# Dealing out anew the preparation of later steps in a three-layer graph network with a closing attention layer

## The chip, the cores and the metric

The kernel runs on one core of a Trainium2 chip. The metric is device time in microseconds of one execution. TensorE is called PE here, VectorE DVE, ScalarE ACT, GpSimd POOL, SyncE SP.

## The reference, cut to what matters

There are 8 graphs of N = 1024 nodes with 256 features and a 0/1 adjacency. Each goes through three layers and one closing attention layer, each step resting on the one before:

```python
h = relu(layernorm(x))                       # raw, at the start
for l in range(3):                           # 24 steps of this kind
    s = leaky_relu(si[:, None] + sj[None, :] + b[l], 0.2)      # si, sj = h @ attn_w[l]
    attn = softmax(where(adj + eye > 0, s, -inf))
    z = layernorm(h + attn @ h) * g1 + beta1
    h = layernorm(z + gelu(z @ W1 + b1) @ W2 + b2) * g2 + beta2
x = x + h
w = relu(layernorm(x)) @ W                   # 8 steps of this kind
out = x + elu(softmax(where(adj == 0, -1e9, leaky_relu(...))) @ w)
```

All is float32 in the inputs; the products of the feed-forward part run as pairs of float16 (a high and a low half).

## The kernel before

`ORDER` lists 32 steps (graph, layer) by hand, so that graphs alternate. A step with layer 3 is a GAT step (6, 10, 14, 18, 22, 29, 30, 31), the others are feed-forward (FFN) steps. Steps 8 to 11, 12 to 15, 16 to 19 and 20 to 23 repeat one pattern. No step waits for an idle machine: while step k runs, the engines prepare step k+1, at times k+2 too. Each engine has its own program in program order, and semaphores tie them together.

One FFN step is, on PE: eight aggregations t = 0 to 7 (`aggregate`: product of the exponentials `pw` with the node values `xx` into the banks OB0 and OB1 by turns, 16 matmuls each), with transposes (`transpose_h` into the bank TH) between them; then sixteen slots n = 0 to 15 with `hidden(n+2)` (6 matmuls into FBB) and `second(n)` (12 matmuls into OB). A GAT step has the eight aggregations alone. On DVE, `residual1(t)` frees OB, `ht_low(j)` makes the low half of a transposed pair and so frees TH, `g_low(n)` makes the low half of the gelu output, which `hidden(n+2)` and `second(n)` wait for, `residual2` takes the result. ACT does `ht_high`, `gelu` (an activation and a copy), the normalisations and exponentials. POOL does the layer norms' scales (`ln_rstd`), `affine` and `final`, the sums into the output.

Preparing a step q takes, in this order: tile scores (`scores(q, t)` on DVE, two operations a tile, lines 1192 and 1197); the score columns, their transpose and copy (`columns`, `transpose_c` into TP, `cT_copy`); `spread_s1` and `spread_sj` on PE, with `r2_copy` on ACT between them; eight row maxima (`row_max` on DVE, line 1250) and after each four the shift columns; eight shifted masks `nms` on ACT (line 919); sixteen units (`unit` on PE: four small products of a mask with the identity into a bank; `score` on DVE, line 1274; `exps` on ACT). Unit u is half u//8 of the nodes, tile u%8. Its bank comes from `score_bank`: R0 and R1 (the halves of RB) by turns, or R0, R1, TH in rotation where `three_banks(q)` holds, as for the GAT steps 10, 14, 18, 22; units 12 to 15 of steps behind a GAT step ("carried", done in the step itself) use TH and TP. A unit in TH waits for the last user of TH to be done (`th_after`).

What stands in which slot is written out in tables: `MAX_*` for row maxima, `SHIFT_*` for masks, `UNITS_*` for units (DVE scores a unit one slot later, `unit_scores`), keyed by slot (t, or 8 + n, or END). `prep_tables` picks them: FE for most steps, FC for steps 9, 13, 17, 21 (in front of a GAT step), FL for late ones, GA for GAT steps in front of an `AHEAD` step (11, 15, 19, 23), TA and TB for the last two. For the AHEAD steps, preparation begins two steps earlier (`MAX_AHEAD`, and the lines with `k + 2 in AHEAD`). `GAT_AT` says in which step the input of an attention layer is prepared: early in 8, 12, 16, 20, 24, 28 (`gat_statistics`, `ln_rstd(LNG)`, `normalise_pair(LNG)`, `gat_transpose`, `gat_low`, `gat_product`, `gat_values`, and `gat_edges`, which puts the diagonal into the mask). In a GAT step, DVE's `elu_a(t)` takes OB, ACT's `elu` makes the exponential and positive part, and POOL's `final` adds both to the output tile; `elu_a(t)` waits for `final(t-2)`.

The lines that the argument touches:

```python
                if t == HT:
                    pe.wait_ge(exp_done, 16 * k + 2 * NT)
...
                    if n in (1, 4) and k not in GAT_FFN_LATE:
                        ht_low(k, 2 + n // 4)
...
                if b == "TH" and th_after:
                    pe.wait_ge(*th_after[-1])
```

## Time and profile before

| | us |
|---|---|
| median of 3 runs | 2446.71 (2444.73 to 2447.41) |
| the profiled execution | 2446.48 |
| its span, first to last instruction | 2444.8 |
| PE busy in it | 2254.4 (92%) |
| DVE busy | 1892.5 (77%) |
| ACT busy | 1572.0 (64%) |
| POOL busy | 1139.1 (47%) |
| mean granted TensorE clock | 0.986 |

The span lies 1.7 us below the execution's own time. The page gives busy times by engine, the span in 40 slices, and the costliest groups of instructions. The view of waits sums for each group how long its engine was idle in front of it and which instruction released it. The order of time lists every instruction, or a merged run of like ones (x16), with its start, its duration and, in brackets, the idle time before it and the releaser. The table of stretches gives each engine's busy time between two times, and the granted TensorE clock (1.00 is 2.4 GHz, half of it 1.2 GHz). Step 12 runs from 1007.9, step 13 from 1096.7, step 14 from 1181.1, step 15 from 1216.3 to 1297.9 us of the span; step 29 begins at 2313.1, step 30 at 2364.6, step 31 at 2409.9.

### The profile page before, as it was taken

How to read it: one execution, taken by the hardware profiler on the slowest of the kernel's cores; microseconds unless marked ns; L12 is line 12 of the kernel's file. 1: busy time of each engine (PE TensorE's matmuls, PEld its weight loads, DVE VectorE, ACT ScalarE, POOL GpSimd, SP SyncE). 2: the span in 40 equal slices, each digit the busy share in tenths (PEclk: the TensorE clock that was granted, in tenths of full speed). 3: DMA queues.
4: the chain of work that ended last, by engine and by line, in shares of the span. 5: the costliest groups of instructions: out<-in, count | busy, mean ns of one | idle time of the engine just before them, and what ended most of it. 6: DMA issues, size and time to landing. Idle time of an engine off the chain costs nothing.

```text
span 2444.8 us, 41401 instructions
## 1 busy us (share of the span) xinstructions
PE 2254.4 (92%) x14623; PEld 1711.6 (70%) x14623; DVE 1892.5 (77%) x5043; ACT 1572.0 (64%) x2450; POOL 1139.1 (47%) x2128
## 2 busy tenths in 40 slices
PE   5889999998899999999899999999998999999988
PEld 4666766776667767767777767777675777677667
DVE  7777778758788887888887788978878677767875
ACT  5467566666666676676766666766656557666754
POOL 3344346354264543644546444554544445335643
PEclk9899999999999999999999999999999999999989
DMA  6312012011130112200121102111131010010000
GB/s 217 120 44 90 6 61 78 11 51 48 48 113 1 44 48 83 78 19 26 64 84 61 44 5 91 60 53 44 40 108 56 6 44 10 5 40 23 23 25 29
DMA packets 66221, 128.55 MB, mean 53 GB/s; under 512 B 12985, under 2 KB 53213, under 8 KB 62942
## 3 DMA queue, kind: packets, MB, share of 16 engines
q1 hardware_dynamic: 66014, 125.90, 15.4%
q8 instruction: 116, 1.90, 0.3%
q14 instruction: 91, 0.75, 0.1%
HBM read 111.20 MB, written 14.68 MB: 51 GB/s over the span
## 4 chain that ended last, share of the span: by engine, by line
PE 61%; DVE 26%; issue 5%; POOL 4%; ACT 3%; DMA 1%; SPq 0%; DVEq 0%; POOLq 0%; ACTq 0%
PE OB L1639 40%; PE FBB L1639 13%; DVE mj L1250 5%; DVE pw L1274 4%; PE RB L1639 4%; DVE gT L1288 3%; DVE st L1141 2%; DVE junk L1192 2%; PE TH L1639 2%; DVE xc L1168 1%; DVE junk L1197 1%; PE TH L1680 1%; POOL xc L676 1%; DVE xc L1155 1%; DMA adjst<-in_adj 1%
## 5 line engine op out<-in xcount | busy, mean ns | idle before, releaser
L1639 PE MATMUL OB<-xx,pw 128*128 128x257 f32 x4096 | 947.2, 386 | 22.7 <-DVE xc L1168 10.9
L1639 PEld LDWEIGHTS OB<-xx,pw 128*128 128x128 f32 x4096 | 770.3, 192 | 149.9 <-DVE xc L1168 16.8
L1639 PE MATMUL FBB<-hT,wb 128*128 128x512 f16 x2304 | 563.1, 383 | 55.1 <-DVE gT L1288 54.3
L1639 PE MATMUL OB<-wb,gT 128*128 128x256 f16 x4608 | 572.4, 275 | 10.1 <-DVE gT L1288 10.1
L1639 PEld LDWEIGHTS OB<-wb,gT 128*128 128x128 f16 x4608 | 453.4, 99 | 141.3 <-DVE gT L1288 12.6
L649 POOL TENSOR_SCALAR ve<-mv 128x2 f32<-128x2 f32 x256 | 59.5, 233 | 1026.5 <-DVE mv L1144 1018.1
L891 ACT ACTIVATE FBB<-FBB,wc 128x512 f32<-128x512 f32 x384 | 252.2, 657 | 292.3 <-PE FBB L1639 291.7
L1639 PEld LDWEIGHTS FBB<-hT,wb 128*128 128x128 f16 x2304 | 214.0, 98 | 265.7 <-DVE gT L1288 66.6
L1288 DVE TENSOR_TENSOR gT<-FBB,gT 128x512 f16<-128x512 f32 x384 | 262.0, 683 | 171.9 <-ACT gT L896 171.7
L902 ACT ACTIVATE pw<-pw,sj 128x512 f32<-128x512 f32 x512 | 334.1, 710 | 59.7 <-DVE pw L1274 58.9
L676 POOL TENSOR_TENSOR xc<-xc,gb 128x256 f32<-128x256 f32 x384 | 292.0, 760 | 33.5 <-ACT xc L866 32.4
L919 ACT ACTIVATE nms<-nm,cc 128x1024 bf16<-128x1024 bf16 x256 | 282.3, 1137 | 19.0 <-DVE cc L1265 19.0
L866 ACT ACTIVATE xc<-xc,nb,rs 128x256 f32<-128x256 f32 x384 | 212.4, 590 | 104.8 <-POOL nb L657 104.5
L1274 DVE SCALAR_TENSOR_TENSOR pw<-r2s,sj,RB 128x512 f32<-128x512 f32 x377 | 268.4, 738 | 3.5 <-PE RB L1639 3.3
L1250 DVE CUSTOM_DVE_ANT_0 mj<-RB,nm 128x1024 bf16<-128x1024 f32 x224 | 267.2, 1215 | 0.0
L896 ACT ACTIVATE gT<-FBB 128x512 f16<-128x512 f32 x384 | 229.3, 597 | 12.1
L654 POOL TENSOR_TENSOR rs<-ve,mhalf 128x2 f32<-128x2 f32 x256 | 183.6, 717 | 21.3
L1151 DVE RECIPROCAL rden<-OB 128x1 f32<-128x1 f32 x192 | 32.0, 166 | 204.7 <-PE OB L1639 203.7
L1639 PE MATMUL RB<-identb,nms 128*128 128x128 bf16 x1508 | 134.9, 224 | 34.8 <-DVE pw L1274 29.3
L1141 DVE BATCH_NORM_STATS2 st<-xc 128x6 f32<-128x256 f32 x392 | 156.7, 421 | 6.8
L678 POOL TENSOR_TENSOR xx<-xc,gb 128x256 f32<-128x256 f32 x192 | 147.8, 770 | 15.1
L1197 DVE CUSTOM_DVE_ANT_0 junk<-xx,aw 128x256 bf16<-128x256 f32 x256 | 154.6, 604 | 0.0
(141 smaller groups left out, 2334.0 us busy)
## 6 DMA issues: line engine op xcount, KB each, us to landing
wb<-w_scratch SPq DMA_DIRECT2D x19, 2048.0 KB, 7.9
adjst<-in_adj SPq DMA_DIRECT2D x56, 512.0 KB, 4.1
xx<-in_x SPq DMA_DIRECT2D x16, 512.0 KB, 5.7
nm<-in_L_gnn_W SPq DMA_DIRECT2D x6, 1024.0 KB, 8.5
gb<-in_L_gnn_g SPq DMA_DIRECT2D x48, 128.0 KB, 2.8
adjst<-in_x SPq DMA_DIRECT2D x6, 1024.0 KB, 10.9
out_x<-adjst SPq DMA_DIRECT2D x48, 128.0 KB, 1.7
pw<-in_adj SPq DMA_DIRECT2D x4, 1024.0 KB, 9.6
```

Source lines behind the costliest of these rows:

```text
L654: pool.tensor_tensor(out=rs[:, kind, c], in0=ve[:, kind, c], in1=mhalf[:, :], op=ALU.pow)\
L676: pool.tensor_tensor(out=v, in0=v, in1=gb[:, 0, :], op=ALU.mult).then_inc(mul_done[kind], 1)
L866: act.activation(dst, src, ACT.Relu if kind in (LNR, LNG) else ACT.Identity, bias=nb[:, kind, t:t + 1], scale=rs[:, kind, t:t + 1])\
L891: act.activation(src, src, ACT.Gelu, bias=b1c[:, layer(k), f:f + 1], scale=1.0 / W_SCALE)\
L896: act.activation(gT[:, i % GRING, 0, :], src, ACT.Copy).then_inc(ghi_done, 1)
L902: act.activation(v, v, ACT.Exp, bias=sj2[:, q % 2, jt:jt + 1]).then_inc(exp_done, 1)
L919: act.activation(nms[:, it, :], nm[:, slot(q), it, :], ACT.Identity, bias=cc[:, it:it + 1])\
L1141: dve.bn_stats(st[:, kind, t % 2, :], src[:, t, 0:D]).then_inc(bs_done[kind], 1)
L1250: dve.tensor_tensor_reduce(out=mj[:, n % 2, :], in0=row_bank(q)[:, :], in1=nm[:, g % 3, t, :], scale=1.0, scalar=-3e38, op0=ALU.add, op1=A ...
L1274: dve.scalar_tensor_tensor(out=pw[:, jt, half], in0=r2s[:, half], scalar=sj8[:, q % 2, jt:jt + 1], in1=b, op0=ALU.max, op1=ALU.add).then_i ...
L1288: dve.tensor_tensor(out=gT[:, i % GRING, 1, :], in0=FB[i % 2][:, :], in1=gT[:, i % GRING, 0, :], op=ALU.subtract).then_inc(glo_odd if n % ...
L1639: return pe.matmul(o, lhsT, rhs, start=first, stop=last)
```

## The change

It is a new dealing of the same work over slots and engines, in these parts.

1. Steps in front of a GAT step (FC): row maximum 5 a slot earlier, masks from the fourth on and all units a slot earlier.
2. AHEAD steps: all eight tile scores in t = 0 to 5 two steps before (four of them were in n = 1, 3, 5, 7), columns, copies, spreads and row maxima a slot earlier, maxima 6 and 7 at the end of that step and no longer in the GAT step; in the GAT step the other tile scores one a tile at first, and the units from t = 3.
3. Unit 13 of an AHEAD step goes to the bank R0; the next step's spread waits for its score.
4. The diagonal masks (`gat_edges`) go from n = 3 into the aggregation, t = 4. POOL's LNG scale comes ahead of the affine operations, ACT's first LNG pair from n = 2 to n = 3.
5. `g_low(2)` directly behind `ht_low(2)` at n = 1; at n = 8 the scores before the residuals.
6. The aggregation waits for each exponential of the second half alone.
7. Step 29: DVE makes the sum of the ELU's two parts (`elu_b`), the last GAT product and its low half come behind the units and their scores, the last exponentials ahead of the last values. Step 30: unit 15 a tile later.

```diff
--- before.py
+++ after.py
@@ -57,6 +57,7 @@
 GAT_AT = {5: 0, 8: 1, 12: 2, 16: 3, 20: 4, 24: 5, 28: 6, 29: 7}
+ELU_DVE = {29}
 LATE = {2, 3, 4, 26, 27, 28}
@@ -88,15 +89,14 @@
 MAX_FE = {2: (0,), 3: (1,), 4: (2,), 5: (3,), 6: (4,), 7: (5,), 8: (6,), 9: (7,)}
-MAX_FC = {2: (0,), 3: (1,), 4: (2,), 5: (3,), 6: (4,), 7: (5, 6), 8: (7,)}
+MAX_FC = {2: (0,), 3: (1,), 4: (2,), 5: (3,), 6: (4, 5), 7: (6,), 8: (7,)}
 MAX_GX = {2: (0, 1), 3: (2, 3), 4: (4, 5), 5: (6, 7)}
...
 MAX_GE = {3: (0,), 4: (1, 2), 5: (3, 4), 6: (5, 6), 7: (7,)}
-MAX_AHEAD = {21: (0,), 22: (1, 2), 23: (3,), END: (4, 5)}
-MAX_GA = {0: (6,), 1: (7,)}
+MAX_AHEAD = {20: (0,), 21: (1, 2), 22: (3,), 23: (4, 5), END: (6, 7)}
 ALL8 = tuple(range(NT))
@@ -107,7 +107,7 @@
 UNITS_FG = {23: (0, 1), END: (2, 3, 4, 5, 6, 7)}
-UNITS_FC = {11: (0, 1), 12: (2, 3), 13: (4, 5), 14: (6, 7), 15: (8, 9), 16: (10, 11), 17: (12, 13, 14, 15)}
+UNITS_FC = {10: (0, 1), 11: (2, 3), 12: (4, 5), 13: (6, 7), 14: (8, 9), 15: (10, 11, 12), 16: (13, 14, 15)}
 MAX_TA = {1: (0,), 2: (1, 2), 3: (3, 4), 4: (5,), 5: (6,), 6: (7,)}
@@ -122,14 +122,14 @@
 UNITS_GE = {END: TO12}
-UNITS_GA = {4: (0, 1), 5: (2, 3), 6: (4, 5), 7: (6, 7), END: (8, 9, 10, 11)}
+UNITS_GA = {3: (0, 1), 4: (2, 3), 5: (4, 5), 6: (6, 7), END: (8, 9, 10, 11)}
...
 SHIFT_FG = {21: (0, 1), 22: (2, 3), END: (4, 5, 6, 7)}
-SHIFT_FC = {6: (0, 1), 7: (2,), 10: (3,), 11: (4,), 12: (5,), 13: (6,), 14: (7,)}
+SHIFT_FC = {6: (0, 1), 7: (2,), 9: (3,), 10: (4,), 11: (5,), 12: (6,), 13: (7,)}
 SHIFT_GE = {6: (0, 1), 7: (2, 3), END: (4, 5, 6, 7)}
@@ -149,7 +149,7 @@
     if v == "ahead":
-        return dict(col=None, ct=None, s1=None, sj=None, row=MAX_GA, units=UNITS_GA, shift=SHIFT_GA)
+        return dict(col=None, ct=None, s1=None, sj=None, row={}, units=UNITS_GA, shift=SHIFT_GA)
     if v == "early":
@@ -176,7 +176,7 @@
     if k == 30:
-        return {1: (8, 9, 10, 11), 2: (12, 13, 14, 15)}
+        return {1: (8, 9, 10, 11), 2: (12, 13, 14), 3: (15,)}
     if k == 31:
@@ -197,6 +197,8 @@
         return ("TH", "TP")[u % 2] if u in (8, 9, 12, 13) else ("R0", "R1")[u % 2]
+    if q in AHEAD and u == 13:
+        return "R0"
     if q in CARRY and u in (8, 9, 12, 13, 14, 15):
@@ -695,9 +697,10 @@
                 v = x1_of(g)[:, t, :]
-                pool.wait_ge(elu_exp, n)
-                pool.tensor_tensor(out=v, in0=v, in1=vn[:, t % 2, :], op=ALU.add).then_inc(elu_sum, 1)
-                pool.wait_ge(elu_max, n)
+                if k not in ELU_DVE:
+                    pool.wait_ge(elu_exp, n)
+                    pool.tensor_tensor(out=v, in0=v, in1=vn[:, t % 2, :], op=ALU.add).then_inc(elu_sum, 1)
+                    pool.wait_ge(elu_max, n)
                 pool.wait_ge(elu_sum, n)
@@ -742,6 +745,8 @@
                         ln_rstd(LNR, raw, n // 2)
+                    if gat is not None and early and n in (1, 3, 5, 7):
+                        ln_rstd(LNG, gat, n // 2)
                     if n in (1, 3, 9, 11):
@@ -758,8 +763,6 @@
                             self_edges(raw, n - 2)
-                    if gat is not None and early and n in (1, 3, 5, 7):
-                        ln_rstd(LNG, gat, n // 2)
                     if n == 12:
@@ -1035,11 +1038,11 @@
                         normalise_pair(LNR, raw, (5, 7, 8, 9).index(n))
-                    if k + 2 in AHEAD and n == 12:
+                    if k + 2 in AHEAD and n == 11:
                         r2_copy(k + 2)
                     if gat is not None and early:
-                        if n in (2, 4, 6, 8):
-                            if n == 2:
+                        if n in (3, 4, 6, 8):
+                            if n == 3:
                                 act.wait_ge(max_done, 8 * (k + 1) + 8)
@@ -1082,11 +1085,9 @@
                     gat_pair(gat, 3)
-                    exps(k + 1, 2)
-                    exps(k + 1, 3)
+                    for u in range(2, NT):
+                        exps(k + 1, u)
                     gat_values(gat, 3)
-                    for u in range(4, NT):
-                        exps(k + 1, u)
                     shifts(k, END)
@@ -1352,6 +1353,14 @@
+            def elu_b(k, t):
+
+                n = 8 * ORDER[k][0] + t + 1
+                dve.wait_ge(elu_exp, n)
+                dve.wait_ge(elu_max, n)
+                dve.tensor_tensor(out=va[:, t % 2, :], in0=vn[:, t % 2, :], in1=va[:, t % 2, :], op=ALU.add)\
+                   .then_inc(elu_sum, 1)
+
             def piece_low(i):
@@ -1379,9 +1388,11 @@
                 elif is_gat(k) and k + 1 in AHEAD:
-                    tiles = {0: (0, 1), 1: (2, 3), 2: (4, 5), 3: (6, 7)}.get(at, ())
+                    tiles = {0: (0,), 1: (1,), 2: (2, 3), 3: (4,), 4: (5,), 5: (6,), 6: (7,)}.get(at, ())
                 elif k + 1 in LATE:
                     tiles = {2: (4, 5), 3: (6, 7)}.get(at, ())
+                elif k + 2 in AHEAD:
+                    tiles = {0: (0, 1), 1: (2, 3), 2: (4,), 3: (5,), 4: (6,), 5: (7,)}.get(at, ())
                 else:
@@ -1445,9 +1456,11 @@
                         gat_statistics(gat, t - 5)
+                    if gat is not None and early and t == 4:
+                        gat_edges(gat)
                 g_low(k, 1)
                 for n in range(NF):
-                    if n > 1:
+                    if n > 1 and (n > 2 or k in GAT_FFN_LATE):
                         g_low(k, n)
@@ -1467,19 +1480,21 @@
                         ht_low(k, 2 + n // 4)
+                    if n == 1 and k not in GAT_FFN_LATE:
+                        g_low(k, 2)
                     if k < 2 and n == 7:
...
                         piece_low(2 * k + n // 14)
+                    unit_scores(k, 8 + n)
                     if n == 8:
...
                             residual2(k, t)
-                    unit_scores(k, 8 + n)
                     prepare(k, 8 + n)
                     if k + 2 in AHEAD:
-                        if n == 8:
+                        if n == 7:
                             columns(k + 2)
-                        if n == 10:
+                        if n == 9:
                             cT_copy(k + 2)
@@ -1509,14 +1524,10 @@
                             gat_low(gat, (n - 5) // 2)
-                        if n == 3:
-                            gat_edges(gat)
                         if n == 13 and gat == 6:
...
                             scores(GAT_STEP[gat], n - 8)
-                    if k + 2 in AHEAD and n in (1, 3, 5, 7):
-                        scores(k + 2, n // 2)
                     if nxt is not None and n >= 14 and k + 2 not in AHEAD and k + 3 not in AHEAD \
@@ -1547,6 +1558,8 @@
                     elu_a(k, t)
+                    if k in ELU_DVE and t >= 1:
+                        elu_b(k, t - 1)
                     if gat is not None and t in (1, 2, 4, 5):
@@ -1566,9 +1579,11 @@
                         gat_sum(7)
+                if k in ELU_DVE:
+                    elu_b(k, NT - 1)
                 if gat is not None:
+                    finish(k)
                     gat_low(gat, 3)
-                    finish(k)
                     for t in range(HT):
@@ -1662,11 +1677,9 @@
                 rows = slice(t * P, (t + 1) * P)
-                if t == HT:
-                    pe.wait_ge(exp_done, 16 * k + 2 * NT)
                 for jt in nodes:
-                    if t == 0:
-                        pe.wait_ge(exp_done, 16 * k + jt + 1)
+                    if t % HT == 0:
+                        pe.wait_ge(exp_done, 16 * k + NT * (t // HT) + jt + 1)
                     ins = mm(o[:, 0:D + 1], pw[:, jt, rows], xx[:, s, jt, 0:D + 1], jt == 0, jt == NT - 1)
@@ -1751,7 +1764,7 @@
                 if q > 0:
-                    pe.wait_ge(x_done, 16 * q - (4 if q - 1 in CARRY and q - 1 not in RB_CARRY else 0))
+                    pe.wait_ge(x_done, 16 * q - (2 if q - 1 in AHEAD else 4 if q - 1 in CARRY and q - 1 not in RB_CARRY else 0))
                 spread(1, row1_done, RB)
@@ -1866,11 +1879,11 @@
                     if k + 2 in AHEAD:
-                        if n == 9:
+                        if n == 8:
                             transpose_c(k + 2)
+                        if n == 10:
+                            spread_s1(k + 2)
                         if n == 11:
-                            spread_s1(k + 2)
-                        if n == 12:
                             spread_sj(k + 2)
@@ -1911,9 +1924,9 @@
                         gat_colsum(7)
+                prepare(k, END)
                 if gat is not None:
                     gat_product(gat, 3)
-                prepare(k, END)
...
             pe.wait_ge(zero_done, 2)
```

## Rows read from the trace of the kernel before

**Rows 1.** The page, engines: busy us (share of the span) x instructions

```profile
PE 2254.4 (92%) x14623; PEld 1711.6 (70%) x14623; DVE 1892.5 (77%) x5043; ACT 1572.0 (64%) x2450; POOL 1139.1 (47%) x2128
```

**Rows 2.** PE waits, whole span: us in total, times, longest

```profile
PE FBB L1639 <- DVE gT L1288: 54.3, 48, 3.9
...
PE OB L1639 <- ACT pw L902: 3.3, 2, 2.5
```

**Rows 3.** Steps 13 and 14: length; busy PE, PEld, DVE, ACT, POOL; clock, DMA, GB/s

```profile
1096.70:1181.10 84.40, 79.99 (x532) 59.17 (x532) 66.74 (x177) 53.66 (x83) 38.64 (x71) 1.00 0.10 32
1181.10:1216.30 35.20, 31.70 (x177) 26.62 (x177) 31.38 (x95) 28.90 (x49) 20.65 (x32) 1.00 0.24 86
```

**Rows 4.** PE waits in step 12 (1007.9 to 1096.7), columns as above

```profile
PE FBB L1639 <- DVE gT L1288: 2.3, 2, 1.9
PE RB L1639 <- DVE pw L1274: 1.4, 1, 1.4
...
PE TP L1798 <- DVE mj L1325: 0.3, 1, 0.3
```

**Rows 5.** Order of time, step 12: start, us, engine, what [idle before <-releaser]

```profile
1048.50 0.68 DVE L1288 TENSOR_TENSOR gT<-FBB,gT 128x512 f16<-128x512 f32 x1
...
1050.25 1.09 ACT L866 ACTIVATE mj<-adjst,nb,rs 128x256 f32<-128x256 f32 x2 [3.79 <-POOL nb L657]
...
1053.35 2.19 DVE L1319 SCALAR_TENSOR_TENSOR nm<-ident,dgm,nm 128x128 bf16<-128x128 f32 x8
```

**Rows 6.** Order of time, PE in step 13

```profile
1104.55 0.61 PE L1639 MATMUL RB<-cT,sel 32*128 32x128 bf16 x8
...
1138.21 1.47 PE L1639 MATMUL FBB<-hT,wb 128*128 128x512 f16 x6 [1.22 <-DVE gT L1288]
...
1143.88 0.39 PE L1639 MATMUL TH<-identb,nms 128*128 128x128 bf16 x4
...
1157.76 0.40 PE L1639 MATMUL TH<-identb,nms 128*128 128x128 bf16 x4 [1.29 <-DVE pw L1274]
...
1162.30 0.40 PE L1639 MATMUL RB<-identb,nms 128*128 128x128 bf16 x4 [0.86 <-DVE pw L1274]
```

**Rows 7.** All of line 1192 (min/median/max ns), then order of time, DVE and ACT

```profile
L1192 DVE CUSTOM_DVE_ANT_0 junk<-xx,aw x256: 407/422/985, 10.2 to 2376.0; 128x256 bf16<-128x256 f32 x128
...
1102.09 0.18 DVE L1225 COPY cT<-TP 64x128 bf16<-64x128 bf16 x1
...
1135.49 0.63 ACT L891 ACTIVATE FBB<-FBB,wc 128x512 f32<-128x512 f32 x1
...
1141.65 0.68 DVE L1282 TENSOR_TENSOR hT<-TH,hT 128x512 f16<-128x512 f32 x1
```

**Rows 8.** Order of time, PE and ACT in step 14

```profile
1181.13 14.16 PE L1639 MATMUL OB<-xx,pw 128*128 128x257 f32 x64 [0.77 <-DVE xc L1168]
...
1194.35 2.17 ACT L919 ACTIVATE nms<-nm,cc 128x1024 bf16<-128x1024 bf16 x2
...
1197.27 3.74 PE L1639 MATMUL OB<-xx,pw 128*128 128x257 f32 x16 [1.98 <-DVE hT L1345]
...
1215.41 0.40 PE L1639 MATMUL RB<-identb,nms 128*128 128x128 bf16 x4 [0.87 <-DVE pw L1274]
```

**Rows 9.** Order of time, PE in step 15

```profile
1221.55 0.40 PE L1639 MATMUL TP<-identb,nms 128*128 128x128 bf16 x4 [1.06 <-DVE cT L1225]
```

**Rows 10.** Order of time, PE in step 26

```profile
2102.78 1.47 PE L1639 MATMUL FBB<-hT,wb 128*128 128x512 f16 x6 [1.03 <-DVE gT L1288]
...
2105.67 1.47 PE L1639 MATMUL FBB<-hT,wb 128*128 128x512 f16 x6
```

**Rows 11.** Order of time, PE in steps 29 and 30

```profile
2359.66 2.74 PE L1639 MATMUL TH<-gw,wb 128*128 128x256 f16 x12 [2.67 <-DVE wb L1325]
...
2379.33 0.40 PE L1639 MATMUL TH<-identb,nms 128*128 128x128 bf16 x4 [2.51 <-DVE pw L1274]
...
2379.83 5.42 PE L1639 MATMUL OB<-xx,pw 128*128 128x257 f32 x16
```

## Prediction

> **What bounds the kernel now.** I read the page first. PE is busy 92% of the span, 190 us short of it [rows 1], so the kernel is a PE stream with holes and a change can gain only what it takes out of the holes. The total of PE's waits then says whose they are: most are waits for DVE (the low half of the gelu output, gT, 54.3 us in 48 waits), 3.3 us in two waits are for ACT's exponentials [rows 2]. The steps repeat: 8 to 11, 12 to 15, 16 to 19 and 20 to 23 are one cycle, which I read at 12 to 15; the table of stretches gives steps 13 and 14 as 84.40 and 35.20 us with PE busy 79.99 and 31.70 [rows 3], so 4.4 and 3.5 us are idle. Then I went through the order of time at each hole. Below, t is an aggregation tile, n one of the 16 slots of the feed-forward part, and a gain is a hole that goes less the hole that comes next. PE, DVE, ACT and POOL each run in program order, so a moved line moves all that stands behind it.
>
> **Steps with an early attention layer in preparation (8, 12, 16, 20, 28; 24 alike).** Before, DVE does the row maximum and the shift columns in front of gT for n=2, at 1048.50, and PE waits 1.9 us for it [rows 4, 5]. ACT stands 3.79 us for POOL's LNG scale in front of gelu 3, then DVE spends 2.19 us on the diagonal masks (eight operations) in front of gT 4 and the first scores, and PE waits 0.4 and 1.4 us more [rows 4, 5]. After: gT 2 comes straight behind hT's low half, at 1046.7, so PE goes on at 1047.2 (1.9 gone). POOL makes the LNG scale ahead of the four affine operations, ACT's pair moves behind gelu 3. But that pair now ends near 1051.2, since gelu 3, one hT copy and a shifted mask (waiting for the shift columns, near 1049.0) stand ahead of it, and PE, at the transposes by 1050.3, waits 0.9. The first scores are ready at 54.4, PE wants a bank at 54.2: 0.25. DVE then reaches the low half of the transposed x late, as before (0.3 of wait [rows 4]), and I put 0.95. Old 1.9+0.4+1.4+0.3 = 4.0, new 2.1: 1.9 each. The masks now lie at t=4, where DVE waited for PE about 1 us a tile: 2.4 us more make the low half for n=0 end at about 36.9 where PE wants it at 36.8, so 0.1 at most; without that cover it would be 2.4. Six steps give 11.4 us. Bounds: 0.5 (the wait only moves, see the rivals) to 2.8 each.
>
> **Steps 9, 13, 17, 21.** Removed: 1.22 (gT 2 stood behind tile scores), 1.29 (the scores of n=8 stood behind the residuals, which wait for PE) and 0.86 (the next bank behind those) [rows 6], 3.37 us. Added, two things. (a) Four tile scores come into t=0 and 1 of DVE, in front of the cT copy, which ends at 1102.3 [rows 7] and which the next spread, at 1104.55 [rows 6], needs. POOL runs its affine operations just then; one such operation takes 0.42 us in the median and up to 0.985 [rows 7], and the long ones lie beside POOL's additions. Two tiles, four operations: about 1.4 us if none is long (they overlap a little), about 2.9 if three are, as in step 14's like stretch. The copy then ends near 1105.2: a wait of 0.65. Behind it on DVE are three constants and the residual of t=1, not wanted soon.
> (b) The units of step 14 are dealt one slot earlier, so unit 2 stands at n=3 in PE. It uses the bank TH, and TH holds the fourth transpose pair until DVE's ht_low(3), which stays at n=4, behind g_low(4). In the trace before, that copy runs at 1141.65 [rows 7] and unit 2 comes at 1143.88 without a wait [rows 6]. After, counting from 1133.3: PE ends second(2) at about 1139.4 and meets unit 2. ACT makes a shifted mask (1.1) at n=2, then gelu 3 (two operations, 1.3), the hT copy (0.6), a mask (1.1), gelu 4 (1.3), from 1135.6 (gelu 3 starts at 1135.49 today, and two masks take 2.17 [rows 7, 8]): 1140.9. Then DVE g_low(4) and ht_low(3), 0.6 each: 1142.1. PE waits **2.7 us** with hidden(5), second(3) and all the rest queued behind it. Bounds: 1.5 (ACT does a mask less in front) and 3.9 (the longest gT wait of the whole trace [rows 2]). Nothing in the diff moves ht_low(3).
> Gone 3.37, come 3.35: zero. But the two waits of this length in the last steps, 2.67 and 2.51 us, are each followed by matmuls at 1.2 GHz, sixteen in 5.42 us [rows 11] instead of the 3.74 of a tile at 2.4 GHz [rows 8]: 1.7 us. Waits of 1.98 and less in this cycle have a full granted clock behind them [rows 3, 8] (step 14's stretch has 1.00). I take 1.7 for all four: **6.8 us lost**; ends 0 and 4 x 3.4.
>
> The Trainium skill's GPSIMD Engine Reference (section Specifications) says that POOL shares its SBUF interfaces with DVE and contends with DVE instructions that have two SBUF inputs, as the tile scores have; it speaks against moving them under the affine operations. The 0.985 beside 0.42 agrees [rows 7]. Without contention (a) is nothing and the sum is 2.6 us lower.
>
> **Steps 10, 14, 18, 22.** Removed: 1.98 us at tile 4, where OB waits for the third elu_a behind two row maxima and four tile scores of DVE [rows 8], and 0.87 at the end, with two of 0.26 beside it (R0 and R1 wait for scores), 3.37 together. Row maxima 6 and 7 go in front of elu_a(0), which no longer delays PE before t=2. Added: PE meets units 0 and 1 after tile 3, at about 1195.5, while ACT ends the shifted mask for rows 2 and 3 at 1196.5 [rows 8]: 0.85. Tile 4 then ends at 1200.5, and units 2 and 3 find their banks free at about 1201.5 and 1202.1, as elu_a(2) waits for POOL's first final until 1194.6 and pushes the scores back: near 0.9 beyond PE's own time. At the start DVE has two row maxima (2.3) in n=15 instead of one and the shift columns (1.8), so the 0.77 in front of tile 0 [rows 8] grows by 0.35. 3.37 - 0.85 - 0.9 - 0.35 = 1.3; by a chain that counts DVE's uncontended times it is 2.1; I take 1.6: 6.4 us. Bounds 0 and 2.2.
>
> **Steps 11, 15, 19.** Unit 13 goes to R0 and no longer waits 1.06 us for cT [rows 9]: 3.2 us. The spread of t=1 now waits for score 13, about 1 us early. Step 23 has no such transpose.
>
> **Step 0 and step 7.** The aggregation waits for each exponential alone. The two waits were 3.3 us [rows 2]; the last two tiles are wanted 2.6 us later than the first, so both go: 3.3. Step 7 also had the longest gT wait, 3.9, in front of n=2; gT 3 stays where it is on DVE, so of it about 1.5 remain gained. 4.8 together; ends 2 and 7.
>
> **Other late steps.** In 2, 3, 4, 25, 26, 27 the wait (1.03 in step 26 [rows 10]) in front of hidden(4) goes as well, but hidden(5) there starts at 2105.67, right behind gT 3 [rows 10], which DVE does no sooner: zero.
>
> **Steps 29 and 30.** In 29 the product waits 2.67 us and runs at half clock [rows 11]; the four units and their scores go in front of it, and what is left is about 1.7 of wait: 2.2 us. ELU sums on DVE (eight at about 0.4) take as many of 0.73 off POOL, whose final holds elu_a back: 0.2. In 30 unit 15 waited 2.51 us in TH for unit 12's score; a tile later it finds the bank free and its exponential is ready 1 us before tile 4 wants it. With the half clock behind it: 2.5+1.7, less 0.3: 3.9. Together 6.3; ends 2 and 8.
>
> **The sum.** 11.4 - 6.8 + 6.4 + 3.2 + 4.8 + 0 + 6.3 = 25.3 us off the profiled execution of 2446.48, whose span of 2444.8 is 1.7 shorter. It is 0.2 below the median of 2446.71, which changes nothing. **2421 us**, 1.0% less.
>
> **Rivals.**
> (1) The wait at unit 2 comes but the clock stays up, as behind the 1.98: +6.8 gained, 2414. For it: 2.7 is close to the limit between the kinds. Against: both waits over 2.5 near the end have the slow stretch.
> (2) The holes only move, as in step 26 [rows 10]: gT 2 is early and PE stands again one slot later, since ACT's gelu 3 and the chain of the transposes set the pace. Six steps give 0.5 instead of 1.9 and step 7 nothing: 2431.
> (3) As (2), and the GAT steps give nothing since ACT, which is busy through tiles 0 to 3, is the bound there: 2437 to 2441, hardly to be told from no change.
> (4) Slower. TH is the bound of steps 9, 13, 17, 21: unit 2 and, one slot on, unit 5 both meet it late, each as long as the longest wait (3.9 [rows 2]) and each with 3.4 us lost to a slow clock twice as long. 2 x 7.3 + 0.65 - 3.37 = 11.9 a step, 47.5 in all against 32.1 of the other terms: 2462. It decides from 8 us a step. Against it: unit 5 only needs score 2, one slot earlier on DVE, which has nothing else there.
>
> **Chances.** The forecast 0.45, (1) 0.2, (2) 0.2, (3) 0.08, (4) 0.07. The range reaches from (1) with the better ends of the GAT steps and of step 30 to (3): 2405 to 2440. What a measurement of this kernel can tell from no change is about 0.2%, 4.9 us: under 2441.8 is faster. Faster 0.87, within 0.07, slower 0.06.
>
> **What would show it.** Right: a PE wait of 2 to 3 us in front of four matmuls TH<-identb,nms at about n=3 of steps 9, 13, 17, 21, with the granted clock of the stretch below 1.00; step 14 near 33.6 us with no wait at tile 4; step 12 near 87; step 15 near 80.5; no wait of PE on TP in it; step 30 four us shorter. Wrong: no wait at TH (then step 13 is 3 us shorter), or a wait before hidden(5) in step 12 as long as the one that went.

## The result and the profile after

The changed kernel takes 2409.22 us (median of 4, 2407.82 to 2414.69) against 2445.72 for the kernel before (4 runs, 2441.23 to 2447.41): a ratio of 0.9865, interval 0.985 to 0.988, 1.35% faster. The profiled execution took 2410.06, so 36.4 us went, where I had 25.3. The page's engine line, to be held against [rows 1]:

```profile
PE 2246.6 (93%) x14623; PEld 1707.8 (71%) x14623; DVE 1896.2 (79%) x5051; ACT 1572.4 (65%) x2450; POOL 1130.3 (47%) x2120
```

PE is still the stream that counts; of the span's 36.5 us 28.7 are idle time gone and 7.8 busy time. Of the busy time 4.6 are half-clock stretches (8.8 us less busy time in steps 5, 7, 24, 29 and 30, 4.2 more in 9, 13 and 17); the rest are 0.1 to 0.4 us in many steps. PE's waits over the whole span (in all, times, longest) say whose idle time it was:

```profile
PE FBB L1654 <- DVE gT L1289: 35.6, 27, 4.0
PE RB L1654 <- DVE pw L1275: 17.9, 30, 4.2
PE OB L1654 <- DVE xc L1169: 13.7, 21, 1.5
...
PE TH L1654 <- DVE hT L1283: 12.1, 5, 2.5
```

The waits for gT fell from 54.3 us in 48 to 35.6 in 27 [rows 2]. New is the last line, of which the kernel before had one wait of 0.4 us: five waits of units for `ht_low`, four of them my wait at unit 2, the fifth in step 7. In the stretches of steps 12, 13, 14, 21 and 23 (length; busy PE, PEld, DVE, ACT, POOL; clock, DMA share, GB/s) the two in the middle answer to [rows 3]:

```profile
993.90:1080.20 86.30, 84.55 (x577) 64.59 (x577) 67.86 (x184) 58.91 (x95) 44.07 (x88) 1.00 0.14 44
1080.20:1166.80 86.60, 81.45 (x532) 59.64 (x532) 70.46 (x181) 54.95 (x85) 38.91 (x71) 0.98 0.11 34
1166.80:1199.50 32.70, 31.32 (x177) 26.65 (x177) 27.76 (x89) 27.61 (x45) 19.22 (x30) 1.00 0.22 87
...
1651.80:1736.80 85.00, 79.83 (x533) 59.14 (x533) 70.45 (x181) 55.01 (x85) 38.93 (x71) 1.00 0.10 35
1769.40:1860.00 90.60, 79.62 (x518) 58.62 (x515) 67.67 (x170) 52.59 (x83) 39.45 (x75) 0.98 0.21 66
```

Step 13 is 2.2 us longer than before and its clock below 1.00; step 14 is 2.5 shorter. Read so from the first aggregation of each step to that of the next, the 36.4 us lie here:

| steps | forecast | measured |
|---|---|---|
| 8, 12, 16, 20 (-2.4 each), 24 (-2.7), 28 (-3.9) | -11.4 | -16.3 |
| 9, 13, 17 (+2.0, +2.2, +2.2), 21 (+0.5) | +6.8 | +6.9 |
| 10, 14, 18, 22 | -6.4 | -10.1 |
| 11, 15, 19 | -3.2 | -3.8 |
| 23 | 0 | +2.4 |
| 0 and 7 | -4.8 | -4.9 |
| 29 and 30 | -6.3 | -5.5 |
| in front of step 0 (-1.7), 3 (-1.8), 4 (-0.8), 5 (-0.9) | 0 | -5.2 |

PE's holes in steps 13 and 14, with what ended them:

```profile
1089.13 0.61 PE L1654 MATMUL RB<-cT,sel 32*128 32x128 bf16 x8 [1.00 <-DVE cT L1226]
...
1126.64 0.40 PE L1654 MATMUL TH<-identb,nms 128*128 128x128 bf16 x4 [2.41 <-DVE hT L1283]
...
1127.17 2.76 PE L1654 MATMUL FBB<-hT,wb 128*128 128x512 f16 x6
...
1166.83 14.16 PE L1654 MATMUL OB<-xx,pw 128*128 128x257 f32 x64 [1.47 <-DVE xc L1169]
1181.42 0.61 PE L1654 MATMUL RB<-identb,nms 128*128 128x128 bf16 x8 [0.43 <-ACT nms L922]
1186.22 0.40 PE L1654 MATMUL RB<-identb,nms 128*128 128x128 bf16 x4 [0.67 <-DVE pw L1275]
```

The three waits of [rows 6] are gone; unit 2 waits 2.41 us in TH, and the six matmuls behind it take 2.76 us instead of 1.47. In step 21 the same wait has the full clock behind it, hence 85.0 instead of 86.6: the stretch costs 1.67 us. At tile 4 of step 14 nothing is left of the 1.98 [rows 8].

In step 7, which the change touches too, the wait of 3.85 us for gT in the kernel before has become two:

```profile
667.57 1.47 PE L1654 MATMUL FBB<-hT,wb 128*128 128x512 f16 x6 [2.36 <-DVE gT L1289]
...
672.85 0.47 PE L1654 MATMUL TH<-identb,nms 128*128 128x128 bf16 x4 [2.50 <-DVE hT L1283]
```

### The profile page after: what moved, and what is told of

Same layout as the page of the kernel before. It is cut to its first block, busy times and chain, and to the rows that moved or that the text cites. A ratio compares the mean times of both kernels' runs of the same rounds, so it can differ in the third digit from the quotient of the medians.

```text
span 2408.3 us, 41405 instructions
## 1 busy us (share of the span) xinstructions
PE 2246.6 (93%) x14623; PEld 1707.8 (71%) x14623; DVE 1896.2 (79%) x5051; ACT 1572.4 (65%) x2450; POOL 1130.3 (47%) x2120
## 4 chain that ended last, share of the span: by engine, by line
PE 55%; DVE 27%; issue 6%; ACT 5%; POOL 5%; DMA 2%; SPq 0%; DVEq 0%; POOLq 0%; ACTq 0%
PE OB L1654 36%; PE FBB L1654 11%; DVE mj L1251 5%; DVE pw L1275 4%; PE RB L1654 4%; DVE gT L1289 3%; DVE st L1142 3%; PE TH L1654 2%; DVE junk L1193 2%; DMA adjst<-in_adj 1%; ACT nms L922 1%; DVE xc L1169 1%; DVE nm L1300 1%; DVE xc L1156 1%; POOL xc L678 1%
## 5 line engine op out<-in xcount | busy, mean ns | idle before, releaser
L1654 PE MATMUL OB<-xx,pw 128*128 128x257 f32 x4096 | 942.5, 385 | 16.0 <-DVE xc L1169 13.7
L1654 PE MATMUL FBB<-hT,wb 128*128 128x512 f16 x2304 | 566.8, 384 | 36.8 <-DVE gT L1289 35.6
L1654 PE MATMUL OB<-wb,gT 128*128 128x256 f16 x4608 | 572.7, 275 | 10.2 <-DVE gT L1289 10.1
L678 POOL TENSOR_TENSOR xc<-xc,gb 128x256 f32<-128x256 f32 x384 | 290.8, 757 | 42.7 <-ACT xc L869 41.9
L680 POOL TENSOR_TENSOR xc<-xc,gb 128x256 f32<-128x256 f32 x192 | 144.3, 751 | 15.1
## 6 DMA issues: line engine op xcount, KB each, us to landing
pw<-in_adj SPq DMA_DIRECT2D x4, 1024.0 KB, 10.4
```

The source lines that it names most:

```text
L678: pool.tensor_tensor(out=v, in0=v, in1=gb[:, 0, :], op=ALU.mult).then_inc(mul_done[kind], 1)
L680: pool.tensor_tensor(out=o, in0=v, in1=gb[:, 1, :], op=ALU.add).then_inc(aff_done[kind], 1)
L1654: return pe.matmul(o, lhsT, rhs, start=first, stop=last)
```

## The experiments

A whole kernel's time moves by 1 to 3 us with the half-clock stretches that it happens to catch, most in steps 0, 3, 5 and 23, and by 1.7 us with the time in front of step 0 (explained in the last section). So I read steps, and beside their length PE's idle time in them. In most steps that a kernel leaves alone, the idle time repeats within 0.2 us. It doesn't in step 0 (12.3 to 13.7), step 3 (8.4 to 9.8), step 5 (10.9 to 11.6), step 6 (3.0 to 3.5), step 11 (2.0 to 2.3) and step 23 (10.4 to 11.6). The four kernels with mixed parts (two sections of undone parts, one of done parts, one last mix) ran once each, at 2424.67, 2416.15, 2434.07 and 2411.97 us in the order of this text, and their steps are read from that one execution.

**Unit 2's bank.** The first theory to test: the wait is for TH, and the slow clock is its consequence.

```diff
-                    if n in (1, 4) and k not in GAT_FFN_LATE:
-                        ht_low(k, 2 + n // 4)
+                    if n in (1, 3 if k + 2 in AHEAD else 4) and k not in GAT_FFN_LATE:
+                        ht_low(k, 2 + (n > 1))
```

> The changed kernel, with DVE's last low half of the transpose pair (the copy that frees bank TH) made one slot earlier (n=3 instead of n=4) in steps 9, 13, 17 and 21 alone. Theory (the wait of 2.41 us in front of unit 2 is for that copy, and the half-clock stretch behind it belongs to that wait): the wait at unit 2 goes to under 0.3 us, the slow stretches of steps 9, 13, 17 go with it, steps 9, 13, 17 are 3.8 to 4.2 us shorter (from 86.4-86.6 to about 82.4), step 21 is 2.2 to 2.5 us shorter (from 84.9 to 82.6), the whole about 14 us shorter: near 2395. Rival A (the copy is a bystander; the hole only moves to the next gT, in front of the hidden product of n=5): the wait at unit 2 goes, another of 1.5 us or more appears within two slots, the steps are at most 1 us shorter, the clock may or may not stay up. Rival B (the slow stretch is not tied to that wait): the steps are 2.4 us shorter, yet a half-clock stretch of the same length still stands in steps 9, 13, 17: near 2400.

2397.92 us, ratio to before 0.9809 (0.979 to 0.983). Steps 9, 13, 17 and 21 take 82.6 us, 3.8, 4.0, 4.0 and 2.3 less: 14.0 in all. The medians differ by 11.3 only; in the profiled executions the time in front of step 0 took 1.7 back. In order of time step 13 has only these two holes and the one of 0.26 before `second`:

```profile
1086.62 0.61 PE L1654 MATMUL RB<-cT,sel 32*128 32x128 bf16 x8 [1.01 <-DVE cT L1226]
...
1160.35 0.92 PE L1654 MATMUL OB<-xx,pw 128*128 128x257 f32 x3 [1.47 <-DVE xc L1169]
```

The theory holds, both rivals fall. With that one line moved the four steps are 7.1 us shorter than in the kernel before; with it left where it was they were 6.9 longer.

**The column copy behind the tile scores.** At slot t=1 of the same steps, with `first = k + 2 in AHEAD and tabs["ct"] == at`:

```diff
+                if first:
+                    cT_copy(k + 1)
+                    constants(k + 1)
                 tile_scores(k, at)
-                if tabs["ct"] == at:
+                if tabs["ct"] == at and not first:
```

> The changed kernel, with DVE's copy of the transposed column sums and the three constants made in front of the two tile scores at t=1 of steps 9, 13, 17, 21. Theory (the wait of 1.00 us in front of the spread of row 1 is for that copy, which stands behind four tile-score operations slowed to 0.9 us beside POOL's affine operations): the wait at the spread falls from 1.00 to under 0.2 us and each of the four steps is 0.8 to 1.0 us shorter, 3.5 to 4 us in all: near 2405.5. Rival (the delay comes back): the tile scores end one or two us later, the score transposes for the next units or the low half of the gelu output are late by the same time, and the steps keep their length within 0.3 us: near 2409.

2407.35 us, 0.9845 (0.983 to 0.986). The wait at the spread is gone and PE's idle time falls from 5.15 to 4.13 us in all four steps; lengths 85.5, then 83.8 three times. So 1.0 a step, as expected; that is read from the idle time, since the medians differ by 1.9 only. That steps 13 and 17 show 2.8 is the slow clock, which did not come this time behind the same 2.41 us. DVE's operations in the changed kernel show why the copy was late:

```profile
1085.62 0.70 DVE L1193 CUSTOM_DVE_ANT_0 junk<-xx,aw 128x256 bf16<-128x256 f32 x1
...
1086.26 0.94 DVE L1198 CUSTOM_DVE_ANT_0 junk<-xx,aw 128x256 bf16<-128x256 f32 x1
...
1087.13 0.94 DVE L1193 CUSTOM_DVE_ANT_0 junk<-xx,aw 128x256 bf16<-128x256 f32 x1
...
1088.87 0.21 DVE L1226 COPY cT<-TP 64x128 bf16<-64x128 bf16 x1
```

POOL runs its affine operations from 1085.32 to 1092.0, and beside them a tile score takes 0.94 us, against the median of 0.42 [rows 7]. Over the whole changed kernel 117 of 512 such operations take more than 0.7 us, and all 117 run beside a POOL operation on two tensors of 256 columns; the 173 that run while POOL is idle take 0.41 to 0.43.

**Step 23, first try.** Statistics and edges of the raw graph's tiles 0 and 1 together at t=1:

```diff
-                        if t % 2 == 0:
-                            raw_statistics(raw, t // 2)
-                        edges(raw, t)
+                        if k == 23 and t < 2:
+                            if t == 1:
+                                raw_statistics(raw, 0)
+                                edges(raw, 0)
+                                edges(raw, 1)
```

> The changed kernel, with DVE's statistics and edge terms of the first raw layer input in step 23 taken at t=1 together, behind the maxima and scores of t=0, instead of at t=0 and t=1. Theory (step 23 grew by 2.4 us because DVE, which runs ahead after the change, meets the raw input before its load has landed, idles 5 us there, and hands the hole on: PE waits 2.33 us at tile 3 and 3.97 in front of a hidden product): DVE's idle time of 5 us goes, PE's wait at tile 3 goes to under 0.5, and step 23 is 2 to 2.5 us shorter (from 90.6 to about 88.3): near 2407. Rival A (the load lands late in any order): DVE idles the same time one tile later, step 23 stays within 0.5 us of 90.6. Rival B (step 23 grew because its other half-clock stretch is longer): the tile-3 wait goes, the step stays at 89.5 or more.

2413.39 us, 0.9873 (0.986 to 0.989). A miss. The wait of 2.33 at tile 3 goes, and DVE waits 1.41 us for the load instead of 4.98, but PE meets another directly behind that tile, and step 23 is 90.2 us (idle 11.03 instead of 10.98):

```profile
1790.72 0.66 PE L1699 MATMUL TH<-ident,xc 128*128 128x128 f32 x4 [3.34 <-ACT xc L869]
```

Rival A holds: the load lands late in any order, and most of the wait only stands elsewhere, on ACT and PE. In the next kernel this edit goes along with the two before and with row maximum 5 at the end of the step:

```diff
-MAX_AHEAD = {20: (0,), 21: (1, 2), 22: (3,), 23: (4, 5), END: (6, 7)}
+MAX_AHEAD = {20: (0,), 21: (1, 2), 22: (3,), 23: (4,), END: (5, 6, 7)}
```

> The changed kernel with the three edits of the runs before it (low half of the pair at n=3, column copy in front of tile scores, raw statistics of step 23 at t=1) and, in steps 9, 13, 17, 21, row maximum 5 of the attention layer moved from slot n=15 to the end of the step, behind what tile 0 of the next step waits for. Theory: the three edits hit different holes, so their gains add: 14 + 3.7 + 2.3 us; the moved maximum takes the wait of 1.47 us in front of tile 0 of steps 10, 14, 18, 22 down to about 0.8, 2.5 us in all: 2409 - 22.5 = near 2387. Rival (the holes are one chain through DVE, and what is taken out of one comes back at the next): less than 14 us in all, near 2396, with a wait at tile 4 of the attention steps of over 1 us that the changed kernel does not have.

2386.99 us, 0.9766 (0.975 to 0.978). Steps 9, 13, 17 and 21 take 80.4 us with 0.7 idle, steps 10, 14, 18 and 22 take 32.35 (32.66 in the changed kernel). The gains add; that step 23 gives nothing is made up for by the tile-0 wait, which falls to 0.32 instead of 0.8.

**One part undone per step.** Since the steps repeat, each can carry its own undone part, and one run gives many differences. In this kernel, among others (ten steps are changed in all):

```diff
-                    if n > 1 and (n > 2 or k in GAT_FFN_LATE):
+                    if n > 1 and (n > 2 or k in GAT_FFN_LATE or k in (8, 12)):
...
-                    if gat is not None and early and t == 4:
+                    if gat is not None and early and t == 4 and k not in (8, 16):
...
-                        if n in (3, 4, 6, 8):
+                        if n in (2 if k in (8, 20) else 3, 4, 6, 8):
...
+                elif k == 22:
+                    tiles = {0: (0, 1), 1: (2, 3), 2: (4, 5), 3: (6, 7)}.get(at, ())
```

> The changed kernel with one part put back in each of ten separate steps, read by the length of each step against the changed kernel's. Theory (each part hits its own hole): step 12 (gT 2 back at n=2) +1.9 us; step 16 (diagonal masks back at n=3) +1.0; step 20 (LNG scale of POOL and first ACT pair back where they were) +0.5; step 8 (all three back) +2.4; step 14 (row maxima 6 and 7 back in front of the first two elu_a) +1.0, made of a shorter wait at tile 0 and a new one at tile 4; step 18 (units one tile later) +0.9 at its end; step 22 (tile scores two a tile) +0.3; step 11 (unit 13 back in TP) +1.0; step 0 (exponentials awaited all at once at tile 4) +1.8; step 29 (elu sums on POOL) +0.2; step 30 (unit 15 back with unit 14) +3.5, with a half-clock stretch. Rival (one chain: the three edits of step 12 work only together): each of steps 12, 16 and 20 alone loses nearly the whole 2.4 us, or each loses under 0.3 and only step 8 the 2.4.

Step lengths against the changed kernel, idle time of PE in brackets:

| step, part undone | expected | measured |
|---|---|---|
| 12, gT 2 | +1.9 | 0.0 (1.77 to 2.02) |
| 16, masks | +1.0 | +0.45 |
| 20, LNG order | +0.5 | +2.8 (1.77 to 4.26) |
| 8, all three | +2.4 | +2.4 |
| 22, tile scores | +0.3 | +3.0 (1.36 to 4.08) |
| 14, row maxima | +1.0 | -0.3; step 13 idle 5.15 to 4.18 |
| 18, units a tile later | +0.9 | +0.1 |
| 11, unit 13 in TP | +1.0 | +1.8 (2.25 to 3.74) |
| 0, exponentials | +1.8 | +0.9 (12.3 to 15.7, untouched up to 13.7) |
| 29, elu sums | +0.2 | -0.7 (7.19 to 6.99) |
| 30, unit 15 | +3.5 | +2.3 (3.21 to 4.40) |

Neither theory nor rival holds: the three edits of step 12 don't share its gain, one has most of it. In step 20, with POOL's LNG scale behind the affine operations again, ACT and PE stand as in the kernel before [rows 4, 5], although gT 2 is early there:

```profile
1615.36 1.09 ACT L874 ACTIVATE mj<-adjst,nb,rs 128x256 f32<-128x256 f32 x2 [3.79 <-POOL nb L662]
```

```profile
1616.50 0.66 PE L1822 MATMUL TP<-ident,mj 128*128 128x128 f32 x4 [1.05 <-ACT mj L874]
1618.40 1.47 PE L1663 MATMUL FBB<-hT,wb 128*128 128x512 f16 x6 [1.24 <-DVE gT L1294]
1622.35 0.40 PE L1663 MATMUL RB<-identb,nms 128*128 128x128 bf16 x4 [1.18 <-DVE pw L1280]
```

In step 12, with gT 2 late, one wait takes the place of the two at TP (0.97 and 0.54) and the step is as long:

```profile
1045.68 1.47 PE L1663 MATMUL FBB<-hT,wb 128*128 128x512 f16 x6 [1.76 <-DVE gT L1294]
```

**A second mix**, with for instance

```diff
+                    if k != 17:
+                        unit_scores(k, 8 + n)
                     if n == 8:
                         for t in range(HT):
                             residual2(k, t)
-                    unit_scores(k, 8 + n)
+                    if k == 17:
+                        unit_scores(k, 8 + n)
```

> The changed kernel with one part put back in each of eight steps, read by step length. Theory: step 13 (units and shifted masks of the next step one slot later) loses the wait of 2.41 us in front of unit 2 and with it any half-clock stretch, and stays under 83.5 us; step 17 (residuals back in front of the unit scores of n=8) +1.3 us; step 9 (row maxima 4 and 5 apart) within 0.2; step 21 (tile scores back at n=1, 3, 5, 7 instead of t=0, 1) loses the 1.00 at the spread and gets 0.5 to 1.2 in front of the hidden products; step 3 (gT 2 back at n=2) +1.8, step 7 +1.9, step 26 within 0.2, since there gT 3 sets the start of the next hidden product in any order; step 29 (PE's product before the units again) +2.0. Rival for step 13: the wait is not for bank TH but for PE's place in a longer chain; then it stands one slot later and the step stays above 85. Rival for step 3: its gain of 1.8 came from elsewhere and it stays at 88.8.

Step 13, units and masks a slot later: the 2.41 goes and no half-clock stretch is left, idle 5.15 to 3.89. The step takes 83.8 us, 0.3 more than I had, for a wait of 0.85 comes at a bank RB. Step 17, residuals in front: +2.6, with a wait of 1.51 and two of 0.26, twice what I had. Step 9: +0.1. Step 21, tile scores back in the slots n: the wait at the spread goes, that at unit 2 grows from 2.41 to 2.99, idle 5.15 to 4.72; with a half-clock stretch behind it the step is 1.0 longer. Step 3, gT 2: length +0.2, which says little there, as its idle time moves by more from kernel to kernel. Steps 7 and 26, gT 2: nothing (-0.05 and 0.0); 26 as forecast, 7 not. In step 7 the wait for gT is 3.86 again and that in TH falls to 0.25. Step 29, the product first again: +1.6 (idle +0.8).

**The raw load, second try.** SP issues it ahead of the attention step's last store; the stores are counted in halves (`out_lo`, `out_done`):

```diff
                     for t in range(NT):
+                        if t == NT - 1 and RAW_AT.get(k + 1, 0) >= 3:
+                            sp.wait_ge(agg_done, 8 * k + 8)
+                            load_x(RAW_AT[k + 1])
+                            sp.wait_ge(out_lo, 64 * (g + 1))
+                            load_adj(RAW_AT[k + 1], 0)
                         sp.wait_ge(o_ready, 8 * g + t + 1)
```

> The changed kernel, with SyncE issuing the load of the next raw graph (and its first adjacency tile) in front of the last store of the attention step's output instead of behind it, after the aggregation of that step; stores counted in two halves so that the first adjacency tile waits only for the first four. Theory (step 23 is 2.4 us longer than before because the changed attention step ends sooner for TensorE while its last output, POOL's, does not, so the load behind that store starts 5.7 us into step 23 instead of 2.3): the load lands 4 to 6 us earlier in step 23, VectorE's idle of 4.98 us is under 1, the wait of 2.33 at tile 3 goes, and step 23 is 2.4 to 3.5 us shorter, under 88.2; steps 7, 11, 15, 19, where the raw input is wanted later, do not change: near 2406.5. Rival (what bounds step 23 is the 3.97 us wait in front of a hidden product, which does not come from the load): VectorE's idle time goes but the step stays above 89.5.

2408.49 us, 0.9854 (0.984 to 0.987). Step 23 takes 86.7 us instead of 90.6, idle 7.71 instead of 10.98; from step 4 on no other step's idle time moves by more than 0.3. The whole kernel shows little of it (0.7 us by the medians). POOL's last output and SP's queue in the changed kernel (step 23 starts at 1769.4), then SP's of this one (at 1772.1):

```profile
1771.13 0.73 POOL L705 TENSOR_TENSOR adjst<-adjst,hT 128x256 f32<-128x256 f32 x1
```

```profile
1771.89 0.33 SPq L599 DMA_DIRECT2D out_x<-adjst  x1
...
1775.08 0.93 SPq L475 DMA_DIRECT2D xx<-in_x  x2
```

```profile
1771.39 0.94 SPq L476 DMA_DIRECT2D xx<-in_x  x2
...
1774.57 0.36 SPq L606 DMA_DIRECT2D out_x<-adjst  x1
```

The load stood 5.7 us into the step and stands 0.7 ahead of it now. DVE, which waited for it in the changed kernel

```profile
1780.78 0.75 DVE L1142 BATCH_NORM_STATS2 st<-xx 128x6 f32<-128x256 f32 x2 [4.98 <-DMA xx<-in_x]
```

has no wait for it left, and PE none at tile 3. The wait in front of `hidden(5)`, 3.98 us, is untouched. So 3.9 us is more than the 2.4 that the change had cost. With the edits at TH, at the copy and at the row maximum, but not the moved statistics:

> The best kernel so far (transpose pair's low half at n=3, column copy first, row maximum 5 at the end of the step), with the earlier raw load in place of the moved raw statistics. Theory: as the kernel with all parts, 2387, less what step 23 gets back, 2.5 to 4 us: near 2383.5. Rival: step 23 keeps its length, 2387.

**2382.54 us** (5 runs, 2380.26 to 2383.22), 0.9744 (0.973 to 0.976) of before, 26.7 us less than the changed kernel: the best version of this study. Its steps 13, 14 and 23:

```profile
1074.00:1154.40 80.40, 79.69 (x532) 59.16 (x532) 68.95 (x179) 53.70 (x83) 38.88 (x71) 1.00 0.10 34
1154.40:1186.80 32.40, 31.26 (x177) 26.61 (x177) 28.31 (x91) 28.56 (x47) 19.55 (x30) 1.00 0.26 94
...
1745.50:1832.20 86.70, 79.00 (x517) 58.68 (x514) 67.50 (x170) 52.64 (x83) 38.79 (x75) 0.98 0.22 69
```

**One part done per step,** on top of the kernel before, so that a part's worth alone and its worth within the change can be told apart. In step 12 POOL's LNG scale ahead of the affine operations, the rest alike:

```diff
+                    if gat is not None and early and n in (1, 3, 5, 7) and k in (8, 12, 28):
+                        ln_rstd(LNG, gat, n // 2)
                     if n in (1, 3, 9, 11):
...
-                        if n in (2, 4, 6, 8):
+                        if n in (3 if k in (8, 12, 28) else 2, 4, 6, 8):
```

> The kernel before, with one part of the change made in each of several separate steps, read by step length against the kernel before (the counterpart of the first mixed kernel, which undid them). Theory A (what undoing showed: the order of the LNG scale carries the gain of the steps with an early attention layer, gT 2 and the masks little): step 12 (LNG order alone) -2.0 to -2.4 us, step 28 (LNG order alone) -2 to -3.9, step 16 (gT 2 alone) within 0.3, step 20 (masks at t=4 alone) within 0.5, step 8 (LNG order and gT 2) as step 12, step 24 and step 3 (gT 2 alone) within 0.5 and about -0.7. Theory B (my prediction's attribution): step 16 -1.9, step 12 -0.5, step 20 -1.0. Further, by undoing: step 22 (tile scores dealt over seven tiles) -2 to -3 with the 1.98 us wait at tile 4 gone, step 14 (units of the next step one tile sooner) within 0.3, steps 17 and 18 (columns and row maxima of the attention layer sooner, 6 and 7 out of the first two elu_a) between -0.5 and +1 together, step 11 (unit 13 in bank R0) -1.0 or more, step 9 (unit scores in front of the residuals) -1.3 to -2.5, step 13 (units and shifted masks sooner, nothing else) +1 to +3 with the wait of 2.4 us in front of unit 2, step 7 (exponentials one by one) -0.8.

| step, the one part | length before | now |
|---|---|---|
| 12, LNG order | 88.81 | 86.78 |
| 16, gT 2 | 88.80 | 88.81 |
| 20, masks | 88.80 | 89.15 |
| 8, LNG order and gT 2 | 88.80 | 86.80 |
| 22, tile scores over seven tiles | 35.16 | 32.58 |
| 14, units a tile sooner | 35.17 | 36.30 |
| 17 and 18, columns and row maxima | 119.57 | 120.03 |
| 11, unit 13 in R0 | 81.51 | 80.43 |
| 9, scores ahead of residuals | 84.41 | 83.09 |
| 13, units and masks a slot sooner | 84.41 | 85.83 |
| 7, exponentials one by one | 94.40 | 91.28 |
| 3, gT 2 | 90.56 | 88.74 |
| 24, gT 2 | 96.68 | 96.67 |
| 28, LNG order | 92.14 | 90.96 |

Theory A holds in steps 8, 12, 16, 20, 22 and 24; B falls. Steps 9, 11, 13 and 17 with 18 lie in their forecasts too, but in step 13 the wait at unit 2 is 1.64, not 2.4, since the 1.22 for gT still stands in front of it, and the clock stays up. Three are misses: step 14 is 1.1 longer, with waits of 1.38 for a mask and 3.15 at a bank RB; step 7 is 3.1 shorter, of which 1.2 are idle time and most of the rest a half-clock stretch that stood behind waits of 1.08 and 0.79 us; step 28 is only 1.2 shorter. Step 3 is 1.8 shorter with gT 2 alone (idle 10.50 to 8.80), more than A had, but undone it had cost only 0.2. In step 28 2.2 us of idle time go and a half-clock stretch comes.

**A last mix of undone parts**: the units of step 22 a tile later, row maxima of 17/18 back, LNG order back in 28 and, with gT 2, in 12, masks back in 24:

```diff
-        return dict(col=None, ct=None, s1=None, sj=None, row={}, units=UNITS_GA, shift=SHIFT_GA)
+        return dict(col=None, ct=None, s1=None, sj=None, row=MAX_GA if q == 19 else {},
+                    units=UNITS_GA0 if q == 23 else UNITS_GA, shift=SHIFT_GA)
```

> The changed kernel with one part put back in each of five places. Theory: step 22 with the next step's first units one tile later again: step 22 within 0.2 us, but step 23 2.0 to 2.5 us shorter, because taking two units out of the end of the step had brought step 23's start 2 us nearer to POOL's last output, behind which the raw load stands (the load is issued 5.7 us into step 23 now, then near 3.5). Rival: the load's lateness comes from the tile scores and stays; step 23 within 0.5 of 90.6. Steps 17 and 18 with the row maxima as before: together 1.0 to 1.3 us shorter (without counting a half-clock stretch, 1.7, that may stand in step 17 or not). Step 28 with the LNG scale's order alone put back: +2.5 to +3.9, the two row maxima of this step included; step 12 with LNG order and gT 2 both put back, masks new: +2.4 to +2.8, all of what step 20 with the LNG order alone showed; step 24 with the masks back: +0.4 if they are what they are in step 16, +2 or more if they carry what the order of LNG, not used in step 24, cannot have brought.

Step 22 +0.1; in step 23 the load is issued 2.3 us in (5.7), and PE's idle time falls from 10.98 to 9.47. The length falls by only 0.6, since a second half-clock stretch stands in the step. So the cause is told apart from the tile scores. Its size, 1.5, shows only in the idle time, which in this step moves by up to 0.6 in kernels that leave it alone. Steps 17 and 18: idle 5.15 to 4.18 and 1.35 to 1.38, so the new row maxima cost 1.0 us a cycle. Step 12 +2.8. Step 28 +3.4, of it 1.6 idle. Step 24 is 1.0 us **shorter** with the masks at n=3 (idle 6.61 to 5.66), outside both cases that I had named.

## Why the prediction was right or wrong

**Step 12 and its like**, 16.3 where I had 11.4 (2.4 each, 3.9 in step 28). The list of waits was right and their owner wrong. I gave 1.9 to gT 2; moved alone it brings 0.0, undone it costs 0.0. The row that I had and priced too low was ACT's 3.79 us for POOL's LNG scale [rows 5]. With that wait, gelu 3 and all behind it are 2 to 3 us late whatever DVE does, and the time that PE gains at gT 2 it gives back at TP and at `hidden(5)`; I had seen just that in step 26 and not carried it over. The LNG order alone brings 2.0, and 2.8 in a kernel with the other two parts in it. The masks bring 0.45 behind that order and cost 0.35 alone. At t=4 of step 24, which I had called alike, they cost 1.0: DVE has row maxima in those tiles, has no idle time from the masks at 1888 until 1905, and PE gets waits of 0.54 and 0.91 us that go when the masks are back at n=3. In the last mix I took the LNG order to have no part in step 24. That was wrong: ACT stood 3.80 us for POOL there before the change and doesn't behind it, and gT 2 alone is worth 0.0 and the masks are a loss, so that order is the likely source of the 2.7. No run moved it alone in this step.

**Steps 9, 13, 17, 21**, +6.9 where I had +6.8: the wait at unit 2, its cause (the bank TH, `ht_low(3)` a slot too late) and the clock behind it came as worked out, 2.41 for 2.7. The copy's wait was 1.00 for 0.65, since all operations behind the first ran slowed. Four at the uncontended 0.42 would have let the copy go near 1087.1 (an estimate), ahead of 1088.1, where PE wanted it. The Trainium skill's GPSIMD Engine Reference (section Specifications) names such pairs of DVE and POOL as contending, and the durations agree (0.94 beside POOL, 0.42 alone). The 1.7 of slow clock came in three steps of four, and the row maxima made the tile-0 wait 0.7 longer, not 0.35. That the sum came within 0.1 of the forecast is luck: the errors in these terms cancel.

**Steps 10, 14, 18, 22**, 10.1 for 6.4, 2.5 each where my bound was 2.2. I put the 1.98 at tile 4 down to the row maxima and the scores in front of elu_a together and took back half of it for banks and masks. Tile scores alone make 2.6 of it; row maxima alone make 0.7 in the GAT step and cost more in the step ahead; units sooner alone cost 1.1. The waits that I let come (0.85 and 0.9) were 0.43 and 0.67.

**Step 23**, +2.4 for 0. I did not follow SP. The units taken out of the end of step 22 bring the start of step 23 nearer to POOL's last output (its end 0.5 us into the step before the change, 2.4 after), and the raw load stands behind that output's store. Of the 3.3 us by which the load is later, 1.9 are this; the rest passes between that store and the load, while SP issues two small loads. The 3.97 in front of `hidden(5)` there, 2.39 and 0.36 before, I have not explained; an earlier load doesn't touch it.

**Steps 11, 15, 19**: right (1.06 of wait; 1.08 alone). **Steps 0 and 7**: right in sum only. The exponentials bring 1.2 idle in step 7. The 1.5 for gT 2 comes as worked out (3.85 to 2.36), but PE gives it back at a unit in TH, 2.50 us for `ht_low`. It is the same collision as in step 13, and I saw it there and not here. A half-clock stretch of 1.7 less makes up for it. Moving `ht_low(3)` forward in step 7 as well is untested. **Steps 29 and 30**: 5.5 for 6.3; the elu sums bring nothing, the order in 29 0.8 and clock, unit 15 1.2 and clock. **Others**, -5.2 where I had 0: step 26 gains nothing, as forecast, but step 3, which I judged by it, gains 1.8; how much of it is gT 2 stays open between 0.2 and 1.8. The 1.7 in front of step 0 is chance, in a piece of code that the change doesn't touch (see the last section). Step 5 takes 96.6 to 99.3 us over the kernels of this study and 97.6 in the kernel before, so its 0.9 says nothing.

**The rivals.** (1), the clock stays up, is true of one step of four. (2), the holes only move, is true of gT 2, but not of the steps, since the LNG order was in the same change. (3) and (4) did not come. Of the signs that I set down, the wait in TH, the clock below 1.00, no wait at tile 4 of step 14, step 12 near 87 (86.4), step 15 near 80.5 (80.2) and no wait on TP in it came; step 14 is 32.7 instead of 33.6 and step 30 3.5 shorter instead of 4. The range held the time, in part by luck. Of the 11.1 us beyond the forecast, 8.6 are errors of one sort in two groups of steps: a part's gain put down to the most visible wait, and part of it taken back for safety. Another 5.2 lie where I had nothing, at least 1.7 of them chance, and step 23 takes 2.4 back.

## What to carry to other kernels

Ask of each wait of the bound engine what would be late next if it were gone, and go up that chain until an engine stands idle: here ACT's 3.79 us for POOL. With that wait in place the two moves on DVE, each alone, were worth nothing (0.0 and a loss of 0.35). When slots of a hand-written order are shifted, check every bank that a shifted user shares with an unshifted one; the line that stayed (`ht_low(3)`) was worth 14 us in four steps, and its like in step 7 went unseen. And when a step gets shorter on one engine, look at what starts by another engine's end: a load in a queue behind a store comes relatively later.
